# Plain fp32 down products, folded last-layer projections and re-timed attention steps in a four-layer transformer kernel

## What is computed

```python
# layer 1 (layer 2 is alike; c gives shift, scale and gate by channel)
q, k, v = split(modulate(ln(x)) @ W_qkv + b_qkv)          # 16 heads of 8
x = x + gate_a * (softmax(q @ k.T * scale) @ v @ W_proj + b_proj)
q_c = ln(x) @ W_qc + b_qc;  k_c, v_c = split(ln(context) @ W_kvc + b_kvc)
x = x + softmax(q_c @ k_c.T * scale) @ v_c @ W_cproj + b_cproj
x = x + gate_m * (gelu(modulate(ln(x)) @ W_mlp1 + b_mlp1) @ W_mlp2 + b_mlp2)
# last layer, p = context rows, a = cond
n = ln(x) * gamma + beta
ev = softmax((n @ Wq) @ (p @ Wk).T / sqrt(128)) @ (p @ Wv)
combined = concat(n, ev, a)
probs = softmax(combined @ router_W + router_b)
expert_e = gelu(combined @ e_w1[e] + e_b1[e]) @ e_w2[e] + e_b2[e]
g = sigmoid(gelu(combined @ gate_w1 + gate_b1) @ gate_w2 + gate_b2)
```

## Time and profile before

| | us |
|---|---|
| median of 3 runs | 3493.57 (3489.97 to 3500.9) |
| profiled execution | 3496.01, of it span 3494.2 |
| layer 0, with setup (same in both kernels) | about 0 to 1408 |
| attention of layer 1 | 1408 to 2104 |
| MLP of layer 1 | 2104 to 2246 |
| attention of layer 2 | 2246 to 2926 |
| MLP of layer 2 | 2926 to 3086 |
| last layer | 3086 to 3494 |

### The profile page before, as it was taken

One profiled execution on the slowest core, in us unless ns is written; L12 is line 12 of the kernel. 1 busy time (PEld: TensorE's weight loads), 2 busy tenths in 40 slices (PEclk: granted clock), 3 DMA queues, 4 the chain that ended last, 5 costly groups with the idle time before them and its releaser, 6 DMA issues. The chain is left out here.

```text
span 3494.2 us, 94730 instructions
## 1 busy us (share of the span) xinstructions
PE 3048.8 (87%) x32127; PEld 2051.7 (59%) x32127; DVE 2754.6 (79%) x12477; ACT 2253.2 (64%) x5572; POOL 1170.7 (34%) x1374
## 2 busy tenths in 40 slices
PE   6999967777777779799999997789999997879999
PEld 3444434444444457566666665556666665568887
DVE  4878779999999978588877759778887776946665
ACT  2666667777777667377766665457776665646665
POOL 0000046666666656311122215521112212532111
PEclk9999979999899889799999999989999999979999
DMA  1111000000000000244444420034444440000000
GB/s 47 44 49 37 14 12 7 9 9 9 8 9 7 3 1 1 72 106 107 107 103 100 104 60 1 20 97 108 106 107 101 105 100 17 1 24 13 11 12 16
DMA packets 139908, 162.90 MB, mean 47 GB/s; under 512 B 41318, under 2 KB 88870, under 8 KB 139174
## 3 DMA queue, kind: packets, MB, share of 16 engines
q1 hardware_dynamic: 127270, 130.80, 14.9%
q0 software_dynamic: 12160, 26.04, 3.2%
HBM read 16.33 MB, written 4.19 MB: 6 GB/s over the span
## 5 line engine op out<-in xcount | busy, mean ns | idle before, releaser
L1374 ACT ACTIVATE attn_pT<-attn_t 128x512 f32<-128x512 f32 (+1 forms) x1024 | 555.7, 597 | 319.7 <-PE attn_t L1631 319.5
L1491 DVE TENSOR_REDUCE attn_mx<-attn_s 128x4 f32<-128x512 f32 (+1 forms) x1024 | 549.4, 578 | 140.2 <-PE attn_s L1616 139.1
L1616 PEld LDWEIGHTS attn_s<-packed_keys,packed_queries 32*128 32x128 f32 x4096 | 276.7, 189 | 161.5 <-DVE attn_mx L1491 96.0
L659 ACT ACTIVATE topk_prob<-topk_s,topk_nmx 128x77 f32<-128x77 f32 x1024 | 248.3, 326 | 181.7 <-DVE topk_work L840 156.0
L1289 POOL DMA_DIRECT2D packed_queries<-attn_om x256 | 142.7, 557 | 645.0 <-ACT attn_om L1367 640.9
L1616 PE MATMUL attn_s<-packed_keys,packed_queries 32*128 32x128 f32 (+1 forms) x4096 | 341.5, 287 | 13.3 <-DVE attn_mx L1491 7.2
L503 POOL TENSOR_SCALAR topk_mask<-topk_work 128x308 f32<-128x308 f32 x256 | 250.1, 977 | 238.9 <-DVE topk_work L845 237.8
L1023 PE MATMUL topk_s<-kbd,topk_qT 128*128 128x308 f32 x512 | 215.4, 505 | 129.7 <-ACT topk_prob L659 129.2
L1656 PE MATMUL attn_o<-attn_pT,attn_vp 128*18 128x128 f32 (+1 forms) x8192 | 326.3, 277 | 0.0
L1631 PE MATMUL attn_t<-packed_queries,packed_keys 32*128 32x128 f32 (+1 forms) x4096 | 299.8, 264 | 0.0
L1870 POOL TENSOR_TENSOR mlp_hid<-mlp_hid 128x512 fp32r<-128x512 f32 x160 | 210.1, 1314 | 156.8 <-DVE mlp_hid L1943 107.9
(11 more groups left out here) (316 smaller groups left out, 7869.7 us busy)
## 6 DMA issues: line engine op xcount, KB each, us to landing
packed_queries<-attn_qT SPq DMA_DIRECT2D x720, 64.0 KB, 2.2
packed_keys<-attn_kT SPq DMA_DIRECT2D x384, 64.0 KB, 2.1
packed_queries<-attn_om POOLq DMA_DIRECT2D x256, 64.0 KB, 2.3
packed_queries<-zero_rows SPq DMA_DIRECT2D x120, 128.0 KB, 2.7
packed_keys<-attn_kT SPq DMA_DIRECT2D x384, 39.0 KB, 2.2
kbd<-window_kT SPq DMA_DIRECT2D x512, 8.0 KB
kbd<-topk_kT SPq DMA_DIRECT2D x512, 4.8 KB
x_res<-in_x SPq DMA_DIRECT2D x16, 192.0 KB, 2.6
```

The source lines that it names most:

```text
L659: last = nc.scalar.activation(prob[:, n % NP, h * keys:(h + 1) * keys], s_ps[:, u % 2, h * keys:(h + 1) * keys], ACT.Exp, scale=SCALE, bia ...
L1374: nc.scalar.activation(pT[0:keys, c % 2, h, :], t_ps[0:keys, h, :], ACT.Exp, scale=SCALE).then_inc(s_exp, 1)
L1491: nc.vector.tensor_reduce(mx[:, (c // 2) % 2, 2 * k + h, :], sc, AX.X, ALU.max).then_inc(s_max, 1)
L1616: last = nc.tensor.matmul(s_ps[:, h, k * KW:(k + 1) * KW], r.qp[32 * j:32 * j + 32, buf, k, b * T:(b + 1) * T], r.kp[32 * j:32 * j + 32, b ...
```

## The change

Three independent parts.

1. **MLP, layers 1 and 2.** The down product is one fp32 product of the unsplit weights with the unsplit `hid`. The casts, the subtractions and the split of w2 are gone; ScalarE's gelu waits for the down product four chunks before, in place of the low part.
2. **Last layer.** The host hands over Wq, Wk and Wv transposed. In the prologue TensorE forms Wq·Wkᵀ (`wqk`) and Wv times the second parts of the expert, gate and router weights, which are split from PSUM. The scores take `n @ wqk` against the context itself; the evidence is taken over raw context rows `v`, which SP loads from HBM, three buffers deep. Keys', values' product and their copies are gone.
3. **Attention, layers 1 and 2.** The projections are in steps 1, 3, 5, 7. The unread products are now (3, 2, 2, 0, 0, 0, 2, 0), at the start of a step, between the wait for both maxima and the scores, into `s_ps`, the scores' own bank. The statistics and normalised rows for group i + 3 are in steps 0, 2 and 4, 6.

```diff
@@ packed_attention_layer
-    XT, KP, QP, VP = 3, 5, 6, 7
+    XT, KP, QP, VP = 1, 3, 5, 7
     ONT, PROJ = 2, 4
-    UNREAD = (2, 3, 2, 2)
+    UNREAD = (3, 2, 2, 0, 0, 0, 2, 0)
...
                     if there(before, left, 3):
+                        if u == 0:
+                            ln_stats(i + 3, (0, 1))
                         if u == 2:
-                            ln_stats(i + 3, (0, 1, 2))
-                        if u == 3:
-                            ln_stats(i + 3, (3,))
+                            ln_stats(i + 3, (2, 3))
                             ln_variance(i + 3)
-                        if u == XT + 1:
+                        if u == 4:
                             ln_apply(i + 3, (0, 1))
-                    if u == 0 and i > 0 and there(before, left, 2):
-                        ln_apply(i + 2, (2, 3))
+                        if u == 6:
+                            ln_apply(i + 3, (2, 3))
...
-            def keep_clock(g, buf, count):
-                pe.wait_ge(s_v, min(g + 2, NT))
+            def keep_clock(buf, count):
                 for _ in range(count):
-                    nc.tensor.matmul(l_ps[:, :], r.kp[:, buf, 0, 0:T], r.kp[:, buf, 0, :], start=True, stop=True)
+                    nc.tensor.matmul(s_ps[:, 0, :], r.kp[:, buf, 0, 0:T], r.kp[:, buf, 0, :], start=True, stop=True)
...
                     if now:
                         scores_waits(i, u)
+                        keep_clock(m3, UNREAD[u] if there(before, left, 2) else 2)
...
-                    if now and u < len(UNREAD):
-                        keep_clock(i, m3, UNREAD[u])
@@ mlp_phase
-                    if swiglu or c < NC - 1:
+                    if swiglu:
                         pool.wait_ge(s_hi, n + 1)
...
-                    if not swiglu:
-                        after(dve, s_down, n - 3)
-                        dve.wait_ge(s_hid, n + 1)
-                        nc.vector.tensor_copy(hid2[:, c, 0, :], hid[:, c % NB, :]).then_inc(s_hi, 1)
...
-                        after(act, s_lo, n - 3)
+                        after(act, s_down, n - 3)
...
+                if not swiglu:
+                    pe.wait_ge(s_hid, n + 1)
+                    nc.tensor.matmul(y_ps[:, par, :], r.W(name, c * C), hid[:, c % NB, :],
+                                     start=(c == 0), stop=(c == NC - 1)).then_inc(s_down, 1)
+                    return
@@ refine_phase
+            for g in range(3):
+                load_values(g)
             for g in range(NG):
                 p = g % 2
+                if there(g + 3):
+                    sp.wait_ge(s_eps, g + 1)
+                    load_values(g + 3)
...
-                nc.tensor.matmul(l_ps[:, 0:K4], r.W("k3"), r.ctxT[:, G * g:G * g + G, :], start=True, stop=True
-                                 ).then_inc(s_kps, 1)
...
+                nc.tensor.matmul(l_ps[:, :], wqk[:, :], nx[:, g % NXB, :], start=True, stop=True).then_inc(s_qps, 1)
...
                     last = nc.tensor.matmul(s_ps[:, b * S:(b + 1) * S], qT[:, b * T:(b + 1) * T],
-                                            kT[:, b * S:(b + 1) * S], start=True, stop=True)
+                                            r.ctxT[:, G * g + b, :], start=True, stop=True)
...
+                for e in range(E):
+                    out = t_ps[:, e * RH:(e + 1) * RH] if e < 2 else u_ps[:, 1, 2 * C:2 * C + RH]
+                    nc.tensor.matmul(out, r.W("v3"), r.W("e1", (e * 3 + 1) * RH, RH), start=True, stop=True)
...
-                if new:
-                    project_values(i + 2)
```

More of the change, by code:

```diff
@@ L1716, in body @@
                         scores_waits(i, u)
+                        keep_clock(m3, UNREAD[u] if there(before, left, 2) else 2)
+                    elif back:
+                        after(pe, s_max, 2 * NS * NT)
+                        keep_clock((m3 + dg) % 3, 2)
                     if back:
@@ L1731, in body @@
                         rows_of_projection(i - 3)
-                    if now and u < len(UNREAD):
-                        keep_clock(i, m3, UNREAD[u])
-                    elif not there(before, left, 2) and (now or back):
-                        keep_clock(i, m3, 2)
                     if there(before, left, 2):
@@ L2140, in spread, with up_part, folded, load_values @@
             return ap.rearrange("p (b a) -> p b a", a=1).broadcast_to([T, G, n])
-        e1_parts = r.W("e1", 0, E * 3 * RH).rearrange("c (e n) -> c e n", e=E)[:, :, 0:2 * RH]
+        e1_first = r.W("e1", 0, E * 3 * RH).rearrange("c (e n) -> c e n", e=E)[:, :, 0:RH]
+        def up_part(p, half):
+            return w1s[:, p, 0:E * 2 * RH].rearrange("c (e n) -> c e n", e=E)[:, :, half * RH:half * RH + RH]
+        def folded():
+            yield t_ps[:, :].rearrange("c (e n) -> c e n", e=2), [up_part(p, 1)[:, 0:2] for p in range(2)]
+            yield u_ps[:, 1:2, 2 * C:2 * C + RH], [up_part(p, 1)[:, 2:3] for p in range(2)]
+            yield g_ps[:, B * E:B * E + C], [w1s[:, p, E * 2 * RH + C:NU] for p in range(2)]
         @block.sync
         def _(sp):
+            def load_values(g):
+                sp.dma_start(v[:, g % 3], r.ctx_v[:, G * g:G * g + G, :]).then_inc(s_vin[g % 3], 16)
             sp.dma_start(r.w3[:, :], io["weights3"]).then_inc(s_w3, 16)
@@ L2304, in prepared @@
                 nc.vector.tensor_copy(arb[:, :, :], by_batch(g_ps[:, 0:B * E], E)).then_inc(s_arb, 1)
+                for k, (product, parts) in enumerate(folded()):
+                    dve.wait_ge(s_fhi, k + 1)
+                    nc.vector.tensor_tensor(parts[1], product, parts[0].bitcast(F32), ALU.subtract).then_inc(s_flo, 1)
             def gate_bias(g):
@@ L2426, in prepare @@
                 act.wait_ge(s_w3, 16)
[L2427 to L2430 removed]
+                nc.scalar.copy(up_part(0, 0), e1_first).then_inc(s_w1hi, 1)
+                nc.scalar.copy(w1s[:, 0, E * 2 * RH:E * 2 * RH + C], r.W("g1", 0, C)).then_inc(s_w1hi, 1)
             def prepared():
@@ L2438, in prepared @@
                                          ).then_inc(s_w2ow, 1)
+                for k, (product, parts) in enumerate(folded()):
+                    if k == 2:
+                        act.wait_ge(s_arb, 1)
+                        nc.scalar.copy(wr[:, :], g_ps[:, B * E + C:B * E + C + E]).then_inc(s_wr, 1)
+                    nc.scalar.copy(parts[0], product).then_inc(s_fhi, 1)
+            act.wait_ge(s_qkps, 1)
+            nc.scalar.copy(wqk[:, :], t_ps[:, 0:C]).then_inc(s_wqk, 1)
             for i in range(-2, NG):
@@ L2477, in transpose_xn @@
             def transpose_xn(g):
-                after(pe, s_v, g)
+                after(pe, s_qT, g)
                 pe.wait_ge(s_xn, g + 1)
@@ L2557, in up @@
                         pe.wait_ge(s_w1lo, 2)
+                        pe.wait_ge(s_flo, 3)
                 after(pe, s_hid, n - 1)
@@ L2595, in down @@
                 last.then_inc(s_dps, 1)
+            nc.tensor.matmul(t_ps[:, 0:C], r.W("q3"), r.W("k3"), start=True, stop=True).then_inc(s_qkps, 1)
             for i in range(-2, NG):
@@ L2614, in _ @@
                     router(i + 1)
-                if new:
-                    project_keys(i + 2)
                 if now:
```

78 lines of the change are left out of this document (33 added, 45 removed).

## The result

The changed kernel takes 3574.8 us (median of four, 3564.4 to 3578.1) against 3493.2 before: ratio 1.0225, interval 1.0198 to 1.0253. It is slower by about 80 us where −9 was forecast, and outside the range. The span grew from 3494.2 to 3575.3 us, and the mean granted clock fell from 0.947 to 0.931.

A forecast was written before the change was run, and what follows sets the result against it. Bounds differed by part: VectorE in the MLP, TensorE in the last layer, neither filling self-attention, where a step chain and SP's packing queue were priced. −37 − 22.5 + 50 = −9.5 us gave 3484 us, range 3460 to 3512.

The forecast's parts named there:

- −37 forecast: MLP of layers 1 and 2: TensorE becomes the bound, group 8.63 to 7.3 us, −18.5 us a layer.
- the old length is 6.67, +0.63: MLP group: TensorE's own length 6.67 us, plus 0.63 for the plain products, gives 7.3 if the transposes hide.
- −22.5 forecast: Last layer: keys' and values' products go, 16 groups give −23 us; prologue set at 0 to +1.
- the cross group of 19.2: Attention, layers 1 and 2: step count for a cross group in the new order, against a mean of 19.50 us before.
- +20: Attention, layers 1 and 2: loss in us in both layers where the packing queue does not bind (groups 21.0 and 19.2).
- cost nothing in such a step: Attention: unread products behind the scores, beside the maxima, cost nothing; ahead of the scores two cost 0.55 us, three 0.78.
- The recursion: Attention's packing queue: landing delays step 7 every second group, periods 21.1 self and 20.3 cross, +50 us in both layers.
- far more than 10 groups: Attention, expected sign: L1355 waits for the queries' DMA in far more than 10 groups a layer, 1 to 2 us each.
- TensorE stays 90% busy: Attention: the argument against rival (4), where unread products no longer hold the clock, 3510 us, chance 0.05.
- the clock a rival: Rival (4), attention: steps 3, 4, 5 and 7 lack unread products, so the clock falls; 3510 us, chance 0.05.
- a granted clock below 0.94 in these stages: Attention and MLP stages: a listed sign that the prediction was wrong; clock before was 0.96 and 0.97 in layer 1.
- Rival (3): Attention, layers 1 and 2: landing holds step 6 itself, so the delay counts in every group; 3538 us, chance 0.12.

The follow-up runs named there:

- the run with two buffers: Kernel before with the MLP and last-layer parts of the change and the old attention, plus two buffers for `qT`: 3411.6 us, ratio 0.977.
- the second buffer: The changed kernel with a second buffer for `qT`, so the queries' copy no longer waits for the last landing: 3495.9 us, ratio 1.000.
- the filler: Two more unread products in step 6 of the changed kernel: 3589.2 us with the landing wait (one `qT` buffer), 3478.2 us with two buffers for `qT`.

## Why the prediction was wrong

**MLP.** −37 forecast, −49 measured. The mechanism held: VectorE was the bound beside GpSimd, TensorE is it now. The mis-sized step is "the old length is 6.67, +0.63". The same group takes 6.63 us in the changed kernel, with the four products each 0.15 longer, so the 6.67 us held some 0.6 us of waiting and were not TensorE's own length. The trace of the kernel before has the wait:

```profile
2234.28 0.47 PE L238 MATMUL mlp_u<-mlp_hT,mlp_w 128*128 128x512 f32 x1 [0.39 <-ACT mlp_hid L1993]
```

It starts 0.79 us after the product ahead of it, where 0.23 is usual. A full group is 7.08 now.

**Last layer.** −22.5 forecast, −20 measured, a group of 21.52 where 21.5 was forecast. The mechanism and the size were right; 16 × 1.41 = 22.6, so some 2 us were lost outside the steady groups, where I had put 0 to 1.

**Attention, the steps.** The self group of 21.0 was measured as 21.16 (undisturbed, step by step 2.77, 2.77, 2.11, 2.30, 2.93, 2.77, 2.45, 3.06), the cross group of 19.2 as 19.41. But the comparison was wrong for cross groups. I set 19.2 against the mean of 19.50 and booked a gain; without landing waits the old order is 18.85, as the run with two buffers shows. The part without landing is (21.16 − 20.08) × 32 + (19.41 − 18.85) × 32 = +52 us in both layers, where I had +20. In the old order of steps the place of the unread products alone costs that much (1.3 and 0.4 us a group). The argument that they "cost nothing in such a step" behind the scores and stand in the way ahead of them held in the old order; in the new one it was worth 0.6 us in a self group and nothing in a cross group.

**Attention, the queue.** The recursion (step 7 not before +23.7 us from the last step 6, every second group) was right in kind and nearly in size: the step 6 of 2566.32 was followed by the step 7 of 2590.42, 24.1 us (23.4 to 26.3 in all disturbed groups), and disturbed and undisturbed groups mostly alternate. The delay by itself was priced a quarter too low: I had +30 for it in both layers, and what the steps 6 exceed their usual length adds up to 42 us (10 in self, 31 in cross groups, where a part of the longest is already at the low clock). But the runs give 79 with the second buffer and 18 more with the filler. L1355 waited 14 times in layer 2 for 24.5 us, against 10 times and 9.3 us before, not in "far more than 10 groups".

**The step that failed** is the dismissal of the clock: "Against: TensorE stays 90% busy." I priced the landing wait by its delay alone. Yet the delay is idle time on TensorE, and behind it 1.5 us (self) to 2.4 us (cross) more are lost at half clock, now and then 10 us. All steps but step 6 exceed their usual length by 63 us in both layers (12 in self, 51 in cross groups), a cost that the sum had at nothing; with the 42 of step 6 this is 105, and the second buffer and the filler together give 97. Part of the falls comes without a landing wait: with two buffers 26 us of such excess stay in cross groups, and the filler removes them. That a fall follows from idle time is shown by the filler: in self groups the delay stayed and the fall went. In cross groups with the landing wait the filler was not enough, and what their falls hang on is not shown. I had made the clock a rival for another reason (no unread products in four steps), at 13 us for a hundredth, with no link to the queue. The granted clock of attention went from 0.97 to 0.92, which that price puts at 65 us, and "a granted clock below 0.94 in these stages" stood among my own signs of being wrong. Rival (3), the slower one, named 3538 us by the right queue and the wrong consequence: the landing did not strike every group.

**The chances.** 0.25 for slower was too little, and the range ended at 3512 because (3) was cut off. With self groups at 21.0 against 20.07 already forecast, only the −59.5 us of the MLP and last layer stood against a loss. They came to −69, without which the miss would have been larger still.

## What to carry to other kernels

Price a new wait twice: what it delays, and what the idle time does to TensorE's clock behind it. A mean over groups that holds an occasional wait is no base for a step count; take the shortest repeated group. When a copy must wait for its old contents to be sent, a second buffer is cheap: with it, the gains of the MLP and last layer, and the old attention, the kernel takes 3411.6 us, 2.3% less than before and the fastest measured here. Nearly all of that is the MLP and last layer (3425.4 us by themselves); in the changed attention the same buffer was worth 79 us.

## What was not expected of the hardware

Idle stretches of TensorE of less than 1 us each (0.94 and 0.34 us in the rows shown) were followed by 3 to 5 us mostly at 1.2 GHz (4.54 us at a mean of 0.62), and several times by a whole group of 30 us (0.58) that repeated nearly to the hundredth: 29.97 in the changed kernel, 29.94 and 29.97 with the filler and the landing wait. From 2791.05 to 2815.00 in the changed kernel TensorE was busy in all of the 23.95 us, and the granted clock was 0.50 throughout. Two 512-column products in idle time removed the falls from the cross groups of a run (19.41 us each). With all unread products gone, groups mostly at full clock and groups mostly at half clock alternated (18.84 and 25.5 us). Why exactly these groups fall is left open: the idle time at L1667 did not decide it.
